# Matrix loads of stages 2 and 3: sixteen transfers of one run of rows from SyncE alone, in place of four over 32 partitions each from SyncE and ScalarE

## What is computed

```python
x_spec = jnp.einsum('nk,nc->kc', adj, x)              # stage 1: adj^T x
coefs  = jnp.exp(-evals * t_eff)[:, None]
y      = jnp.einsum('nk,kc->nc', adj, coefs * x_spec)  # stage 2: adj (coefs * spectrum)
x      = layernorm(x + y)
adj_hat = adj + eye(N); deg = sum(adj_hat, axis=1)
out    = tanh((adj_hat / deg) @ (x @ W) + b)           # stage 3: graph convolution
return layernorm(x + out)
```

## Time and profile before

| | |
|---|---|
| median of 3 runs | 615.78 us (615.32 to 616.95) |
| the profiled execution, its time | 615.71 us |
| its span, first to last instruction | 613.9 us |
| PE busy | 579.9 us (94%) |
| DVE busy | 511.1 us (83%) |
| ACT busy | 399.2 us (65%) |
| POOL busy | 378.2 us (62%) |
| moved by DMA | 174.67 MB, mean 285 GB/s |
| first issue of a load of stages 2 and 3 | 170.2 us from the span's start |

### The profile page before, as it was taken

The page is one execution under the profiler, slowest core; times in us unless marked ns, Lnnn a source line. Parts: engine busy times, 40 slices in busy tenths (PEclk is TensorE's granted clock), DMA queues, the critical chain, the costliest instruction groups (busy, mean ns, idle before and its releaser), DMA issues.

```text
span 613.9 us, 7999 instructions
## 1 busy us (share of the span) xinstructions
PE 579.9 (94%) x2460; PEld 447.1 (73%) x2460; DVE 511.1 (83%) x572; ACT 399.2 (65%) x855; POOL 378.2 (62%) x223
## 2 busy tenths in 40 slices
PE   5999999999998999989999999999999979899993
PEld 5888888888875656758888788887888856656561
DVE  4799999999898988888899799696776768989992
ACT  4999999999996746356555654555444635554552
POOL 0000000000147878788999999879887898997892
PEclk9999999999999999989999999999999999999997
DMA  8999999999999999799979999296995499999101
GB/s 306 408 409 408 410 408 409 409 410 407 410 271 346 328 330 341 212 259 269 242 209 260 254 305 272 66 256 192 256 258 142 123 342 347 348 339 316 35 18 52
DMA packets 125065, 174.67 MB, mean 285 GB/s; under 512 B 6884, under 2 KB 105700, under 8 KB 125032
## 3 DMA queue, kind: packets, MB, share of 16 engines
q1 hardware_dynamic: 72608, 121.68, 59.2%
q10 hardware_dynamic: 52424, 52.58, 30.6%
HBM read 172.13 MB, written 2.11 MB: 284 GB/s over the span
## 4 chain that ended last, share of the span: by engine, by line
PE 60%; POOL 22%; DVE 9%; DMA 3%; issue 3%; ACT 2%; ACTq 1%; DVEq 0%; POOLq 0%
POOL lo L483 18%; PE ps L833 9%; PE ps L835 9%; PE ps L834 9%; PE ps L861 8%; PE ps L863 8%; PE ps L862 8%; PE ps L857 7%; DVE vt L690 5%; DMA raw<-in_adj_dram 2%; DVE lo L697 2%; POOL rstd L462 2%; PE ps L818 1%; ACTq L368 1%; POOL raw L476 1%
## 5 line engine op out<-in xcount | busy, mean ns | idle before, releaser
L483 POOL TENSOR_TENSOR lo<-vt,hi 128x1024 fp32r<-128x1024 f32 x126 | 317.6, 2546 | 31.8 <-ACT hi L538 31.2
L690 DVE STREAM_TRANSPOSE vt<-raw 128x1024 f32<-128x1024 f32 x184 | 222.0, 1226 | 63.1 <-PE ps L863 52.1
L538 ACT ACTIVATE hi<-vt 128x1024 fp32r<-128x1024 f32 x159 | 165.8, 1060 | 128.6 <-DVE vt L690 104.6
L671 DVE TENSOR_TENSOR lo<-raw,hi 128x1024 fp32r<-128x1024 f32 x124 | 156.3, 1265 | 19.1 <-ACT hi L524 10.2
L524 ACT ACTIVATE hi<-raw 128x512 fp32r<-128x512 f32 x256 | 158.9, 623 | 7.2 <-PE ps L835 4.0
L436 POOL TENSOR_TENSOR lo<-raw,hi 128x1024 fp32r<-128x1024 f32 x4 | 10.2, 2556 | 170.7 <-ACT hi L524 170.7
L861 PE MATMUL ps<-hi,s_hi 128*128 128x512 f32 x224 | 94.5, 422 | 7.6 <-POOL lo L483 5.7
L833 PE MATMUL ps<-hi,xg_hi 128*128 128x512 f32 x256 | 100.2, 392 | 1.5 <-DVE lo L671 1.4
L834 PE MATMUL ps<-lo,xg_hi 128*128 128x512 f32 x256 | 99.6, 389 | 0.0
L835 PE MATMUL ps<-hi,xg_lo 128*128 128x512 f32 x256 | 99.6, 389 | 0.0
L861 PE MATMUL ps<-hi,p_hi 128*128 128x512 f32 x206 | 88.1, 428 | 6.9 <-POOL lo L483 6.9
(11 more groups left out here) (69 smaller groups left out, 537.5 us busy)
## 6 DMA issues: line engine op xcount, KB each, us to landing
raw<-in_adj_dram SPq DMA_DIRECT2D x63, 1024.0 KB, 14.3
raw<-in_adj_dram SPq DMA_DIRECT2D x90, 512.0 KB, 9.7
raw<-in_adj_dram ACTq DMA_DIRECT2D x88, 512.0 KB, 11.8
late_raw<-in_adj_dram SPq DMA_DIRECT2D x8, 512.0 KB, 12.6
late_raw<-in_adj_dram ACTq DMA_DIRECT2D x8, 512.0 KB, 14.5
xn<-in_x_dram SPq DMA_DIRECT2D x8, 256.0 KB, 14.0
x_sb<-in_x_dram SPq DMA_DIRECT2D x8, 256.0 KB, 13.7
out_dram<-x_sb ACTq DMA_DIRECT2D x7, 256.0 KB, 2.9
```

The source lines that it names most:

```text
L483: nc.gpsimd.tensor_tensor(lo[:, slot(p), :], vt[:, slot(p), :], hi[:, slot(p), :].bitcast(f32), ALU.subtract).then_inc(pool_lo_ready, 1)
L538: nc.scalar.activation(hi[:, slot(s), :], vt[:, slot(s), :], ACT.Copy).then_inc(hi_ready, 1)
L671: nc.vector.tensor_tensor(lo[:, q % RING1, :], raw[:, k, 2 * h:2 * h + 2, :].rearrange("p r n -> p (r n)"), hi[:, q % RING1, :].bitcast(f3 ...
L690: nc.vector.transpose(vt[:, slot(s), :].rearrange("p (m a i) -> p m a i", m=2, a=RB), load_buffer(st.load).rearrange("p (a m e i) -> p e m ...
```

## The change

SP alone issues every load of stages 2 and 3, as 16 transfers. Transfer `a` writes run `a` of all 128 partitions, 128 KB. Its destination is 128 partitions by 256 elements. Its source is `adj_q[...][:, :, a]`, whose dimensions are q, n, w: 4 steps of 256 elements, in each 32 steps of a matrix row (4096 elements), in each 256 elements in a row. All of ACT's transfers of loads go away. `landed` counts 16 x 16 for each load in place of 16 x 4. The number of 1 KB pieces, the buffers and the waits for them, and every computing instruction stay as they were.

```diff
+    RUNS = 16
...
-    LATE_LOADS = [n for n in range(NL) if LOADS[n].buf >= BUFS and BEFORE[n] is None]
...
-        return 16 * QN * sum(1 for m in range(n + 1) if LOADS[m].buf == LOADS[n].buf)
+        return 16 * RUNS * sum(1 for m in range(n + 1) if LOADS[m].buf == LOADS[n].buf)
...
-        def load_quarters(eng, n, quarters):
+        def load_run(eng, n, a):
+
             ld = LOADS[n]
-            for q in quarters:
-                eng.dma_start(load_buffer(n)[q * QP:(q + 1) * QP].rearrange("p (a w) -> p a w", w=WQ),
-                              adj_q[ld.group // 2, ld.group % 2, ld.wide, q]).then_inc(block_in[ld.buf], 16)
+            eng.dma_start(load_buffer(n)[:, a * WQ:(a + 1) * WQ],
+                          adj_q[ld.group // 2, ld.group % 2, ld.wide][:, :, a]).then_inc(block_in[ld.buf], 16)
...
             for n in range(NL):
                 wait_buffer(sp, n)
-                load_quarters(sp, n, (0, 1))
+                for a in range(RUNS):
+                    load_run(sp, n, a)
...
-                more_loads(s)
...
-            def more_loads(s):
-
-                n = STEP[s].load
-                if s == LAST_STEP[n] and n in BEFORE:
-                    load_quarters(act, BEFORE.index(n), (2, 3))
...
-            late_quarters(0)
```

More of the change, by code:

```diff
@@ L551, in _ @@
                 visit1(2 * d + 2, 0, d + 2)
-            def late_quarters(n):
-                wait_buffer(act, n)
-                load_quarters(act, n, (2, 3))
             def split_spectrum(k):
@@ L571, in _ @@
                 chunk1(LAST, k)
-            late_quarters(0)
             chunk1(LAST, 4)
             chunk1(LAST, 5)
-            late_quarters(1)
             split_spectrum(0)
@@ L578, in _ @@
             chunk1(LAST, 6)
-            late_quarters(2)
             chunk1(LAST, 7)
@@ L583, in _ @@
             hi_step(0)
-            late_quarters(3)
             hi_step(1)
@@ L645, in _ @@
                     ending3(row, since3(p, row))
-                for i, n in enumerate(LATE_LOADS):
-                    if p == END2[LAST] + LAG + 2 + 2 * i:
-                        late_quarters(n)
             act.wait_ge(stored, 16 * (NG + 1))
```

## The result

| | before | after |
|---|---|---|
| median | 616.37 us (615.32 to 618.59, 4 runs) | 1261.96 us (1261.75 to 1262.35, 4 runs) |
| ratio to before | | 2.049, 95% interval 2.044 to 2.055 |
| span of the profiled execution | 613.9 us | 1259.6 us |
| mean granted clock of PE | 0.989 | 0.761 |

The kernel takes twice as long. The direction, the place and the mechanism are those of the prediction (four of the 16 engines do the moving). The time is not: 1262 us lies under the stated range of 1320 to 2100, 8% under the predicted 1367.

The account below looks back on a forecast made before the run. Load transfers on four engines were taken as the bound: 174 us start + 48 x 24.2 = 1160 of loads + 7 for `x` and degrees + 24.4 at the end = 1365, with 1.8 around it 1367 us; range 1320 to 2100.

Parts of the forecast that it names:

- A way of loading that takes more than about 8 us becomes the bound: Stages 2 and 3: loads are issued one each 8.0 us; slower loading bounds all that follows, faster loading stays hidden.
- Four engines: Load transfers of stages 2 and 3: source begins with a count of 4, so 4 of 16 engines work; chance 0.58 unhindered.
- the 772 ns worked out from `ev_t`: SP's load issues: 542 + 230 ns each if a source in few parts costs more to issue, 12.4 us a load.
- Rate of an engine: 21.7 GB/s, 47 ns a piece: Load transfers: each working engine moves 1 KB pieces at 21.7 GB/s, so four give 87 GB/s, 24.2 us a load.
- The row of 215 GB/s: 433 to 435 us: ACT's transfers to partitions 64 to 127, nothing else under way; engines occupied but hindered, 13.4 GB/s each.
- The buffers add nothing: Loads of stages 2 and 3: waits for buffers add no time, since two more loads always stand in the queue.
- The transfers of `x`, the degrees: SP's load queue: the 8 transfers of `x` add 6 us and the degrees 1, together 7 us.
- After the last landing 24.4 us: End of the kernel: the work after the last load lands takes 21.3 us, plus 3.1 for PE at half clock.
- PE would be busy less than half, its clock fall: PE from 170 us on, a sign of four engines: busy less than half the time, with its clock falling.
- Rival: four engines that share a way in, 0.27, 2084 us: Load transfers: four engines hinder each other some or all of the time, at 54 GB/s; chance 0.27.
- Rival: sixteen engines, SP's issue the bound, 623 us: SP's queue: all engines work, each issue takes 0.542 us, 623 us; chance 0.10, including a limit of 215 GB/s.
- Rival: not slower, deciding at 0.50 us an issue: SP's load issues: at 0.311 us each, hidden under 8.0 us a load; ACT saves 6 us, 610 us; chance 0.05.

Follow-up runs that it names:

- e8: Changed kernel with each of SP's sixteen transfers a load reading a plain source, 128 rows of one 1 KB piece (other matrix pieces read): 620.56 us, ratio to before 1.0083.
- e1: Changed kernel with each transfer's source walked rows first, 32 rows by 4 pieces, so pieces land in other partitions: 719.01 us, ratio to before 1.166.
- e4: Changed kernel with each transfer's source read as 2 steps of 64 rows, partly other elements: 2300.91 us in one run.
- e5: Kernel before, with SP alone issuing all loads of stages 2 and 3 as the old four quarters in order: 693.75 us, ratio 1.123.
- e10: Kernel before, with SP issuing quarters 0 and 2, ACT 1 and 3: 676.55 us in three runs, ratio 1.100; 689.50 to 691.80 us in three more.
- e6: Kernel before, with SP alone issuing four transfers a load, each over all 128 partitions, partly other elements read: 614.01 us, ratio 0.9963.
- e7: Kernel before, with four transfers a load over all 128 partitions, two by SP and two by ACT, partly other elements read: 614.46 us, ratio 0.9960.
- e3: Changed kernel with each transfer's source read as 8 steps of 16 rows, partly other elements: 745.77 us, ratio to before 1.210.

## Why the prediction was wrong, point by point

- *A way of loading that takes more than about 8 us becomes the bound.* Right, and e8 measured the edge: 7.9 us a load cost 0.8%.
- *Four engines.* Right. Not shown by any row of before; e1 to e4 show it. What I named for it in the trace did not hold: `ev_t`'s issue was 230 ns dearer, and I took that for a sign that few parts cost more. The shortest issues were 0.503 us with 2 parts (e4), 0.528 with 4, 0.596 with 8 and 0.534 with 32, which shows no such trend. So the right choice rested on the argument that work is cut along the first dimension, and on the cited rule; and the 772 ns worked out from `ev_t` has nothing behind it.
- *Rate of an engine: 21.7 GB/s, 47 ns a piece.* **This is the step that failed.** I took the rate of an engine among 16 for that of an engine among 4, allowed 3% for it, and named 348 GB/s as proof that pieces of 1 KB go no faster. That row says only what 16 do together. Four did 97 to 98 GB/s, 24.3 each, so a piece takes 42 ns and a load 21.9 us by the landings: the first turn of load 0 was at 197.3 us, that of load 47 at 1235.5, and (1038.2 - 7) / 47 = 21.9. 48 x (24.2 - 21.9) = 110 us, and with it the forecast would have been 1257. I even had the other end in hand, 25.5 GB/s with pieces of 4 KB in stage 1, and left it out of the bounds as another kind of piece. As the range's end it would have given 4 x 25.5 = 102 GB/s, 20.6 us a load, 1194 us.
- *The row of 215 GB/s.* The reading is right: the 435 packets of that stretch are all of ACT's queue. But "nothing else is under way" means only that nothing else moved; SP's two transfers for the other half and one of `x` had been issued at 431.94 and 432.83 us and were waiting.
- *The buffers add nothing.* Right: SP's load line waits for nobody.
- *The transfers of `x`, the degrees.* 7 us taken as they stood; not measured apart.
- *After the last landing 24.4 us.* The span ended 24.1 us after the first turn of load 47 began. Right, the clock's part included: the first six matmuls there take 0.43 us, the last six 0.23.
- *PE would be busy less than half, its clock fall.* 39% busy at clock 0.68 from 220 to 400 us, but 51% at 0.74 from 400 to 700; 47% over all from 170 to 1235. A granted clock between 0.5 and 1 in such a stretch is a mixture of the two levels: the same matmul takes 0.43 us in some places and 0.23 in others.
- *Rival: four engines that share a way in, 0.27, 2084 us.* Nothing of it shows; this weight drew the range upwards, on the wrong side. The rule of the halves is real (e5, e10), but it did not slow the four engines: 24 GB/s each is the same with 2, 4 and 8.
- *Rival: sixteen engines, SP's issue the bound, 623 us.* e1 is this rival, and it takes 719: the issue is 0.66 us with its pause, not 0.542. Even with all engines the change would have lost 17%. So of the 646 us lost, 102 are the issue's, had there been 16 engines, and 543 the missing engines'.
- *Rival: not slower, deciding at 0.50 us an issue.* The edge was right, but the gain of 6 us behind it was not: e6 and e7 give ACT's issues no price.

## What to carry to other kernels

Look at the first count of a transfer's source: here it decided how many DMA engines worked, and 4 there left 97 of 347 GB/s, with SP alone and with two issuers. (Sizes other than 128 KB and the count on the SBUF side were not varied.) When a rate falls, read it with the share beside it: a low share means too few engines or too slow an issue; a full share means that the engines are occupied, and then the rate tells how well, 347 GB/s with both halves of the partitions written and 211 to 222 with one. Where a transfer can reach only one half, let two queues write different halves. And a rate divided by the number of workers is a bound for one of them only from below, as long as it isn't known whether the workers or something that they share sets it.

## What the runs showed of the hardware

- An engine moves pieces of 1 KB at 24 to 25 GB/s when 2, 4 or 8 work, and at 21.8 when 16 do (349 GB/s in all, e6), with one queue or with two, as long as both halves of the partitions are written.
- An issue on SP, back to back, takes 0.43 us in the plain form (128 rows) and 0.60 in a nested one (32x4 in e1, 8x16 in e3), with a pause on top: 0.49 and 0.66 us from one to the next in e8 and e1. When the queue is full the row of a load's issue grows to whatever the engines need, 1.28 us with one issuer and 2.60 with two.
- Two queues on the same half of the partitions are hardly faster than one: 218 GB/s (e10, in one of its slower executions) against 211 (e5).
- Each load transfer brings as many packets under 512 B as its source's first count, up to 16: 5348, 6884, 9956 and 16100 of them for 2, 4, 8 and 32.
